# A two-stage vision kernel: probability transposes cut to 113 by 113, the convolution's image pairs written out without a loop, and one wait in the opening moved forward

## What is computed

```python
h = relu(bn(conv1x1(x, w1), g1, b1, m1, v1))
h = relu(bn(conv3x3(h, w2, groups=32), g2, b2, m2, v2))
x = relu(bn(conv1x1(h, w3), g3, b3, m3, v3) + x)          # layer 0

y = roll(layernorm(x) * norm1_w + norm1_b, (-3, -3))       # layer 1
win = y in windows of 7 x 7                                # (B * 64, 49, 128)
q, k, v = split(win @ qkv_w.T)
attn = softmax(q @ k.T * scale + bias + mask)
x = x + roll(merge(attn @ v) @ proj_w.T + proj_b, (3, 3))
z = gelu((layernorm(x) * norm2_w + norm2_b) @ fc1_w.T + fc1_b) @ fc2_w.T + fc2_b
return x + z
```

## Time and profile before

| | |
|---|---|
| median of 3 runs | 4525.73 us (4525.11 to 4525.87) |
| the profiled execution's own time | 4518.32 us |
| its span, first to last instruction | 4516.2 us |
| PE busy | 4423.1 us, 98% of the span |
| ACT, DVE, POOL busy | 76%, 70%, 49% |
| convolution, with the opening | up to about 745 us |
| strips | from there to the end |
| mean granted TensorE clock | 0.992 |

### The profile page before, as it was taken

How to read it: one execution, slowest core, us unless ns; L and a number is a source line. 1 busy time by engine, 2 the same in 40 slices (tenths; PEclk the granted TensorE clock), 3 DMA queues, 4 the chain that set the end, 5 groups by cost and what they waited for, 6 DMA issues and landing times.

```text
span 4516.2 us, 192181 instructions
## 1 busy us (share of the span) xinstructions
PE 4423.1 (98%) x71190; PEld 3178.5 (70%) x71190; DVE 3178.4 (70%) x7717; ACT 3415.4 (76%) x5644; POOL 2207.9 (49%) x3242
## 2 busy tenths in 40 slices
PE   8999996999999999999999999999999999999998
PEld 5666665677777777777777777777777777777775
DVE  4444444777777777777777777777777777777775
ACT  3444443888888888888888888888888888888886
POOL 4444442455554545455555555455555545455553
PEclk9999998999999999999999999999999999999999
DMA  4545442011111111111111111111111111111110
GB/s 138 153 151 163 151 153 66 25 30 29 29 29 30 30 29 29 29 30 29 29 29 30 30 29 29 29 30 29 29 29 29 29 29 29 30 30 29 29 29 26
DMA packets 298330, 218.64 MB, mean 48 GB/s; under 512 B 43377, under 2 KB 245518, under 8 KB 298190
## 3 DMA queue, kind: packets, MB, share of 16 engines
q1 hardware_dynamic: 294632, 215.41, 16.4%
q10 hardware_dynamic: 3558, 1.07, 0.1%
HBM read 110.73 MB, written 111.94 MB: 49 GB/s over the span
## 4 chain that ended last, share of the span: by engine, by line
PE 97%; DVE 1%; issue 1%; ACT 0%; POOL 0%; DMA 0%; DVEq 0%; POOLq 0%; ACTq 0%
PE bank L666 16%; PE bank L608 10%; PE bank L585 8%; PE bank L509 6%; PE bank L576 6%; PE bank L641 6%; PE bank L657 6%; PE bank L595 6%; PE bank L567 5%; PE bank L620 5%; PE bank L522 5%; PE bank L631 4%; PE bank L659 4%; PE bank L658 4%; PE bank L673 2%; PE bank L487 2%
## 5 line engine op out<-in xcount | busy, mean ns | idle before, releaser
L1234 POOL TENSOR_TENSOR sc<-sc,mx 128x784 f32<-128x784 f32 x512 | 779.2, 1522 | 940.9 <-DVE mx L1068 940.9
L666 PE MATMUL bank<-g,fc_sb 128*128 128x392 f32 x2048 | 785.4, 506 | 0.1
L1221 POOL TENSOR_TENSOR res<-x,projb 98x512 f32<-98x512 f32 x256 | 326.3, 1275 | 804.2 <-DVE x L1104 804.2
L861 ACT ACTIVATE g<-bank,fc1b 128x392 f32<-128x392 f32 x1024 | 560.6, 592 | 172.6 <-PE bank L659 172.6
L1087 DVE SCALAR_TENSOR_TENSOR xn<-x,lnp 98x128 f32<-98x128 f32 x1024 | 292.8, 349 | 491.1 <-POOL lnp L1157 491.1
L608 PEld LDWEIGHTS bank<-ident_sb,sc 128*113 128x113 f32 x4096 | 495.6, 177 | 113.1 <-DVE shared L1038 109.8
L666 PEld LDWEIGHTS bank<-g,fc_sb 128*128 128x128 f32 x2048 | 348.7, 190 | 306.2 <-issue 163.1
L608 PE MATMUL bank<-ident_sb,sc 128*113 128x128 f32 x4096 | 547.8, 277 | 0.1
L1062 DVE TENSOR_TENSOR sc<-bank,shared 128x392 f32<-128x392 f32 x1024 | 528.7, 560 | 2.8 <-PE bank L595 2.8
L1068 DVE TENSOR_REDUCE mx<-sc 128x16 f32<-128x784 f32 x512 | 496.6, 970 | 18.5
L1157 POOL TENSOR_TENSOR lnp<-lnp,half 98x8 f32<-98x8 f32 x518 | 467.7, 924 | 20.3
(11 more groups left out here) (105 smaller groups left out, 8258.3 us busy)
## 6 DMA issues: line engine op xcount, KB each, us to landing
x<-x_scratch SPq DMA_DIRECT2D x768, 49.0 KB
out_x<-y SPq DMA_DIRECT2D x672, 49.0 KB
xc_even<-in_x SPq DMA_DIRECT2D x128, 196.0 KB
shared<-in_x SPq DMA_DIRECT2D x128, 196.0 KB
x_scratch<-xc_even SPq DMA_DIRECT2D x128, 196.0 KB
x_scratch<-shared SPq DMA_DIRECT2D x128, 196.0 KB
x<-x_scratch SPq DMA_DIRECT2D x256, 38.5 KB
out_x<-y SPq DMA_DIRECT2D x224, 38.5 KB
```

The costliest lines, as they stand in the source:

```text
L666: mm = nc.tensor.matmul(RC[:, 0:ST], fc2[:, c, :], g[:, c], start=c == 0, stop=c == HC - 1)
L861: nc.scalar.activation(g[:, j], ring[:, 0:ST], ACT.Gelu, bias=fc1b[:, j:j + 1]).then_inc(out_, 1)
L1234: P.tensor_tensor(out=s_r, in0=s_r, in1=m_r.to_broadcast([128, 2 * HEADS, N]), op=ALU.subtract).then_inc(sub_done, 1)
```

## The change

The transposes of the probabilities read only partitions 0 to 112 of `sc`, and stream only 113 columns of the identity, so that each is 113 by 113. The loop over pairs is gone: all 16 periods stand one after the other in the programs of PE, DVE, ACT and POOL, with constants in place of registers. PE's wait at the end of `fill` is for the steps ahead of `fc1_scaled`.

```diff
@@ def over_pairs(e, fill, period): @@
     fill()
-    with e.Fori(0, (BPAIRS - 2) // 2) as k:
-        period(2 * k, 0)
-        period(2 * k + 1, 1)
-    period(BPAIRS - 2, 0)
-    period(BPAIRS - 1, 1)
+    for gp in range(BPAIRS):
+        period(gp, gp % 2)
@@ PE, fill @@
                 bias_steps(8)
-                pe.wait_ge(prep, len(PREP))
+                at(pe, "fc1_scaled")
@@ PE, probs_t @@
                 for q in range(QUADS):
-                    mm = nc.tensor.transpose(RB[j % 2][0:VT, 128 * q:128 * q + 128],
-                                             sc[:, t.u, q, j].rearrange("p h m -> p (h m)")[:, 0:VT], ident[:])
+                    mm = nc.tensor.transpose(RB[j % 2][0:VT, 128 * q:128 * q + VT],
+                                             sc[0:VT, t.u, q, j].rearrange("p h m -> p (h m)")[:, 0:VT],
+                                             ident[0:VT, 0:VT])
                 mm.then_inc(b_full[j % 2], 1)
```

## The result

| | before | after |
|---|---|---|
| median | 4526.10 us (6 runs, 4525.11 to 4528.05) | 4491.75 us (6 runs, 4488.64 to 4496.96) |
| ratio | | 0.9924, 95% interval 0.9911 to 0.9937 |
| profiled execution, span | 4518.3 us, 4516.2 us | 4488.8 us, 4486.7 us |
| PE busy | 4423.1 us | 4407.2 us |

What follows compares the result with a forecast made beforehand. PE was taken to bound strips and convolution. Transposes -18 us, convolution -10, opening -1 sum to -29 us: profiled execution 4518.3 to 4489 us, median 4496 us. Own range 4486 to 4506 (60%), wider range 4474 to 4516.

Steps and rivals of the forecast that it cites:

- The transposes alone: Strips, `probs_t` on PE: 113 instead of 128 columns bring the spacing of transposes from 0.109 to 0.099 us.
- nearly twice: `probs_t` spacing: the trace's 109 ns for 128 columns against the 56 ns of the Trainium skill's formula.
- The reason given for 0.099: `probs_t` spacing: loading 113 columns, 0.11 x 113 / 128 = 0.099 us, is later than streaming's 0.097 us.
- The rival of half pace for an odd number of columns: Transposes: half-pace streaming for odd column counts would cost over 100 us; chance 2%; attend's 49 columns cited against it.
- The first pair gives nothing: `probs_t` 0 and 1, ahead of `hidden` 0: PE waits for DVE's `zt_lo`, so shorter transposes give 0 us.
- The second pair is paid in full: `probs_t` 2 and 3, ahead of `mlp_out` 0: seven distances shrink, 0.07 us a strip, 18 us over 256 strips.
- The loop: Convolution, loop over pairs: pauses fall from 31.4 to 19 us, with 2.0 us for the first conv2 apart; 10.4 us saved.
- The opening: PE's wait before the first conv2: conv2 can start 1.9 us earlier, of which 1 us is counted as saved.
- The slow stretch of the clock stays where it is: First conv2: the half-clock stretch doesn't move, so the 1.9 us earlier start gives back about 1.0 us.
- written-out code hardly pauses: Rival, convolution: all conv2s run at 7.94 us and the 19 us of pauses go too; -46 us, 4480 us; 15%.
- both pairs pay: Rival, strips: the transposes of `probs_t` 0 and 1 save another 18 us too, 4478 us; 7%.
- the slow one: Rival, convolution: written-out code starves, every conv2 pausing 2.1 us as in gp 14; 4539 us; 5%.

Runs made afterwards that it cites:

- `zt_hi` first: Changed kernel with ACT's `zt_out` ahead of `v_out` and `probs_t` 1 ahead of 0; first pair's transposes at 113 columns: 4520.0 us, at 128: 4521.8 us.
- hidden 1 first: Changed kernel, hidden 1 ahead of hidden 0, `q_out` ahead of `zt_rest`, gelu 1 first: 4529.0 us; first pair at 128 columns: 4528.4; gelu 0 first again: 4494.4.
- the run with the stores split: Changed kernel with SP issuing two of a strip's five y stores ahead of the five loads, the other three behind them: 4467.0 us, ratio 0.9868.
- the boundaries moved: Changed kernel with ten one-column fp32 matmuls and one transpose added at the start of PE's program: 4490.9 us, ratio 0.9931.

## Why the prediction came out as it did

**The transposes alone** were right in size: 0.96 us for eight, spaced 0.099 us (0.95 to 0.98 forecast). The last distance, which was to keep 0.11 us, shrank too (872 - 80 = 792), but 13 ns came back in the group behind, so that 67 ns remain for the 70 forecast. The Trainium skill (TensorE: Matmul & The Clock Gate, Back-to-back issue gap) gives 6 ns less for each transpose by its formula for isolated matmuls, 48 ns a group, and the trace has 80. The same section of the Trainium skill gives about 81 ns for 128 columns where each matmul has its weight load, as here; "nearly twice" in the prediction holds against the formula alone, and the trace has 109 ns.

The reason given for 0.099 does not stand. 0.11 x 113 / 128 is 0.097; 0.099 comes out only with the unrounded 0.112 us between the one-column matmuls. And loaded columns did not set the pace of the z and `xn` transposes, which load 128 each; timeline before:

```profile
2001.89 0.37 PEld L567 LDWEIGHTS bank<-ident_sb,xn 98*128 98x128 f32 x4
```

Four such loads take 0.37 us, and of their four matmuls the last three start 84 ns apart, not 112. What goes with the distance in all transposes here is the 98, 113 or 128 of the streamed columns (84, 99 and 109 ns), but the rows that the load reads are the same number each time, and the edit cut these from 128 to 113 as well. No run cuts one alone, so which of the two gives the 10 ns stays open. The rival of half pace for an odd number of columns is out, at 99 ns for 113. Its row was misread by a little: 16 groups have 15 distances, 0.047 us each and not 0.044, and the row shows no even number beside it.

**"The first pair gives nothing"** was right in size: -1 us within 4. The wait ahead of the load was misread, though: from matmul to matmul it was only 0.01 us before (120 ns where the pace is 109), not 0.08, and 0.09 after, so PE and `zt_lo` were nearly level. That `zt_lo` is the reason is supported by the 0.12 us from its end to the load, the same before and after, and by the 41 ns that hidden 1's third matmul waited when the wait for `zt_lo` was put there. That the first pair would pay once nothing holds PE was not shown: in each variant another job came in its place, or took back what the pair gave.

**"The second pair is paid in full"** is the step that failed in size: 18 us forecast, 11 in the trace and 10 in the run with it alone. I followed the saved time up to `row_sums` and stopped. The next place where PE waits is the projection, for DVE's `ot`. Already before, 503 ns stood there for matmuls that need 439; after it is 539, because `ot` doesn't follow PE fully. The likely reason is SP's stores. They follow POOL and the loads, not PE, so that they fall later against attend when PE gets there sooner: the fifth is issued 0.55 us after attend starts before and 0.62 after, with `ot` at 1.057 and 1.076. The runs with `zt_hi` first and with hidden 1 first fit in: 0.44 and 0.39 us, `ot` at 1.013 and 0.983. That is a correlation over traces. What the run with the stores split shows is that stores taken away from attend let `ot` start 0.1 us sooner.

**The loop.** The mechanism was right (boundaries every 256 instructions, 43 earlier in each step, back after six) and the sum a little off: 14 us of pauses for 19 forecast, 15.0 with the loop written out alone (16.4 less the clock's 1.4) and 15.8 with the boundaries moved. The term that was mis-sized is 2.1 us for each step with a boundary at conv2's start: over five such steps of the changed kernel it was 1.5, 0.4, 1.0, 0.1 and 2.2 us, 5 us together for 10.5 forecast. I had one sample of it, gp 14. The Trainium skill (Runtime: NRT & Kernel Launch, Instruction fetch mechanics) calls the crossing mostly hidden; inside conv2 the trace shows it at up to 1.45 us.

**The opening.** "The slow stretch of the clock stays where it is" failed. It followed the idle time that the wait itself made, 2.1 to 2.5 us in five traces, and went with it in eight of nine. The first conv2 took 8.4 us instead of 9.9, and its start came 3.4 us earlier, of which 1.4 are a matter of the clock from 30 to 38 us in that execution (3.4 less the 2.05 between openings of the same clock, for 1.9 forecast). In the runs with the wait alone the whole change is -1 us within 4, which can't be told from zero.

**The median.** I moved the profile's offset of 7.4 us over unchanged; it belongs to PE's loop over pairs. With one profiled execution of each kernel, the loop cost 21 us in the runs and 14 in the profile. What the loop does in an execution that isn't profiled can't be read from a trace, and stays open.

The errors cancelled: strips gave 7 us less than forecast, pauses 5 us more, the opening 4 us more, the last pair 2 us less. That 4489 came out to the microsecond is luck, and so is part of what made it up: 1.4 us of the opening, the last pair, and pauses near the low end of what written-out kernels show. The rivals "written-out code hardly pauses" and "both pairs pay" did not happen, nor did the slow one.

## What to carry to other kernels

Follow a saved time all the way round to where it started, and compare each distance on the bound engine with what its own instructions need: one that is longer is a hidden wait, even where no idle is listed. A pair of traces with one small edit shows where time is given back. And a queue that nobody waits for, SP's stores here, can be worth more than twice what the transposes gave: 25 us, against 10 to 11, for issuing two of five stores in a gap.

## What the hardware showed that I hadn't expected

- Issues or transfers of SP beside attend delay a DVE instruction that waits only for PE, by 0.1 us a strip in the mean of the changed kernel. The y stores' issue and their traffic were moved together; which of the two does it was not tested.
- A profiled execution can hide a cost. With PE's loop of seven rounds, other executions of four kernels are 7 to 8 us longer than the one profiled; in ten kernels without it there is no such offset.
- Pauses at the boundaries of PE's program stand within a matmul of the predicted place, but last from nothing to 1.45 us at the same place (the last 30 to 34 matmuls of steps 4, 10, 16, 22 and 28 of the changed kernel).
